# Gated linear attention beside routed experts: the state update with values stationary on column halves

## The reference, cut to what matters

```python
def step(state, inp):
    qt, kt, vt, at = inp
    state = at[..., None, None] * state + kt[..., None] * vt[:, :, None, :]
    out_t = jnp.einsum('bhk,bhkv->bhv', qt, state)
    return (state, out_t)
```

## Time and profile before

| what | value |
|---|---|
| time, median of 3 runs | 1334.08 us (1331.32 to 1335.56) |
| time of the profiled execution | 1335.15 us |
| its span (first to last instruction) | 1333.5 us |
| mean granted TensorE clock | 0.999 |

### The profile page before, as it was taken

One profiled execution on the slowest core, in us unless ns is written; L12 is line 12 of the kernel. 1 busy time (PEld: TensorE's weight loads), 2 busy tenths in 40 slices (PEclk: granted clock), 3 DMA queues, 4 the chain that ended last, 5 costly groups with the idle time before them and its releaser, 6 DMA issues.

```text
span 1333.5 us, 27468 instructions
## 1 busy us (share of the span) xinstructions
PE 1287.1 (97%) x9460; PEld 1128.6 (85%) x9460; DVE 956.0 (72%) x2431; ACT 550.2 (41%) x1075; POOL 484.4 (36%) x405
## 2 busy tenths in 40 slices
PE   6999999999999999899999999999999999999999
PEld 4888888888888887698888888988988989989887
DVE  6887878889796659866667577576675766757744
ACT  5665555556563433333333333333333333333322
POOL 1110100010010039626455456364554554545530
PEclk9999999999999999999999999999999999999999
DMA  6566534263352212246476476565765766656656
GB/s 228 188 232 185 182 110 164 91 198 116 131 179 73 80 48 80 77 117 150 114 181 162 103 196 133 141 157 122 174 159 109 190 128 159 155 127 157 159 154 229
DMA packets 124919, 194.66 MB, mean 146 GB/s; under 512 B 12016, under 2 KB 98608, under 8 KB 124592
## 3 DMA queue, kind: packets, MB, share of 16 engines
q1 hardware_dynamic: 94384, 147.99, 34.1%
q0 software_dynamic: 30464, 45.83, 19.2%
HBM read 148.62 MB, written 57.74 MB: 155 GB/s over the span
## 4 chain that ended last, share of the span: by engine, by line
PE 72%; DVE 14%; issue 6%; DMA 4%; POOL 2%; ACT 1%; DVEq 0%; SPq 0%; another core or an unknown queue 0%; POOLq 0%; ACTq 0%
PE bank L708 19%; PE bank L809 6%; PE bank L791 6%; PE bank L758 5%; PE bank L723 5%; PE bank L841 5%; PE bank L740 5%; PE bank L776 4%; PE bank L779 4%; PE bank L850 4%; DMA arena<-table,idx_all 3%; PE bank L749 3%; PE bank L831 2%; POOL sel_all L596 1%; PE bank L652 1%
## 5 line engine op out<-in xcount | busy, mean ns | idle before, releaser
L564 POOL DMA_INDIRECT arena<-table,idx_all x132 | 145.7, 1104 | 287.2 <-DVE arena L1458 256.1
L572 POOL DMA_INDIRECT acc<-arena,idx_all x128 | 211.4, 1651 | 43.8 <-issue 41.5
L708 PE MATMUL bank<-xp,wq 128*128 128x512 f32 x768 | 213.3, 413 | 0.0
L708 PE MATMUL bank<-xp,wk 128*128 128x512 f32 x768 | 204.7, 402 | 0.2 <-DVE wk L1274 0.2
L708 PEld LDWEIGHTS bank<-xp,wk 128*128 128x128 f32 x768 | 141.5, 189 | 34.5 <-DVE wk L1274 0.6
L708 PEld LDWEIGHTS bank<-xp,wq 128*128 128x128 f32 x768 | 139.9, 188 | 28.4 <-issue 0.5
L1353 DVE TENSOR_TENSOR_SCAN Dt<-decay,eye_b 128x512 f32<-128x512 f32 x128 | 158.0, 1236 | 0.8 <-issue 0.8
L1029 ACT ACTIVATE qT<-bank 128x512 f32<-128x512 f32 x128 | 76.6, 599 | 144.2 <-PE bank L708 137.4
L758 PE MATMUL bank<-qT,kT 128*128 128x128 f32 x1024 | 135.2, 275 | 0.0
L791 PEld LDWEIGHTS bank<-V,kw 128*128 128x128 f32 x960 | 117.7, 191 | 11.7 <-issue 9.8
L791 PE MATMUL bank<-V,kw 128*128 128x64 f32 x960 | 126.9, 275 | 0.0
(11 more groups left out here) (157 smaller groups left out, 2241.1 us busy)
## 6 DMA issues: line engine op xcount, KB each, us to landing
decay<-decay_dram SPq DMA_DIRECT2D x64, 512.0 KB
carry<-decay_dram SPq DMA_DIRECT2D x60, 512.0 KB, 4.5
arena<-in_L_attn_x_dram SPq DMA_DIRECT2D x16, 512.0 KB, 4.5
table<-arena SPq DMA_DIRECT2D x16, 512.0 KB, 3.4
xT_dram<-arena SPq DMA_DIRECT2D x16, 512.0 KB, 3.0
arena<-in_L_ffn_w_gate_dram SPq DMA_DIRECT2D x64, 128.0 KB
arena<-in_L_ffn_w_up_dram SPq DMA_DIRECT2D x64, 128.0 KB
arena<-in_L_ffn_w_down_dram SPq DMA_DIRECT2D x64, 128.0 KB
```

The lines of the kernel that those rows point to most:

```text
L564: pool.indirect_dma_start(out=xg[:, e % 2, j, :], out_offset=None, in_=table[:, :], in_offset=bass.IndirectOffsetOnAxis(ap=idx_all[:, e, j ...
L572: pool.indirect_dma_start(out=acc[:, :], out_offset=bass.IndirectOffsetOnAxis(ap=idx_all[:, e, j:j + 1], axis=0), in_=yb[:, e % 2, j, :], ...
L708: last = mm(to[:, :], w[:, part, k, h * DK:(h + 1) * DK], xp[:, other, k, :], start=(k + i == 0), stop=(k == KD - 1 and i == 2))
```

## The change

The update is done once for each pair, in the even slot, and turned. V (64 columns) is now stationary, on the column half of its head, and the weighted keys of both heads (`kw` now has room for two) move, 128 columns each. The sum of a pair comes out with values on partitions, in `bank[3]`. ScalarE copies it to SBUF (`update_copy`, into the half of `kw` that the second head has just left free), and TensorE transposes it back into `bank[6]` with four transposes (`update_back`). VectorE adds it as before, with the axes in another order.

On TensorE `update` stands ahead of `outputs`, `update_back` behind it; the odd slots have no update. In the steps "norm" (from step 1) and "count" the projection of the output gate (`proj_og`) moves from between the two projections of a head to behind them. On ScalarE `update_copy` stands behind the copy of the keys, ahead of place 2, except in the experts' steps, where it stands behind the hidden layer's gate, and the high parts of the next weights come after it.

```diff
-        kw = sb("kw", [P, B, DK])
+        kw = sb("kw", [P, 2, B, DK])
+        added_t = kw[:, 1, :, :]
...
                 if not (isinstance(c, int) and c == 0 and h == 0):
                     pe.wait_ge(kw_cp, at(c, 8, h))
+                    if h % 2 == 0:
+                        pe.wait_ge(ut_cp, at(c, 4, h // 2))
...
-            def update(c, h):
-                pe.wait_ge(kw_cp, at(c, 8, h + 1))
-                if h > 0 and h % 2 == 0:
-                    pe.wait_ge(state_up, at(c, 4, h // 2))
-                if h == 0 and not (isinstance(c, int) and c == 0):
+            def update(c, p):
+
+                pe.wait_ge(kw_cp, at(c, 8, 2 * p + 2))
+                pe.wait_ge(v_cp, 4 * c + 4)
+                for b in range(B):
+                    for u in range(2):
+                        h = 2 * p + u
+                        last = mm(bank[3][u * DV:(u + 1) * DV, b * P:(b + 1) * P], V[:, b, h * DV:(h + 1) * DV],
+                                  kw[:, u, b, :], start=True, stop=True)
+                last.then_inc(ut_ps, 1)
+
+            def update_back(c, p):
+
+                pe.wait_ge(ut_cp, at(c, 4, p) + 1)
+                if p > 0:
+                    pe.wait_ge(state_up, at(c, 4, p))
+                elif not (isinstance(c, int) and c == 0):
                     pe.wait_ge(wo_cp, 4 * c)
                 for b in range(B):
-                    lo = (h % 2) * B * DV + b * DV
-                    last = mm(bank[6][:, lo:lo + DV], kw[:, b, :], V[:, b, h * DV:(h + 1) * DV],
-                              start=True, stop=True)
-                if h % 2:
-                    last.then_inc(u_ps, 1)
+                    last = tr(bank[6][:, b * P:(b + 1) * P], added_t[:, b, :], ident[:, :])
+                last.then_inc(u_ps, 1)
...
-                    if s in og_slots(kind):
+                    og_first = first or in_turns(kind)
+                    if s in og_slots(kind) and og_first:
                         proj_og(c, kind, og_slots(kind).index(s))
...
                     if s < H:
                         proj_qk(c, kind, s, 1)
+                    if s in og_slots(kind) and not og_first:
+                        proj_og(c, kind, og_slots(kind).index(s))
                     beside(c, kind, s, 2)
+                    if s % 2 == 0 and not is_last(c):
+                        update(c, s // 2 - 1)
                     if s % 2 == 0:
                         outputs(c, s // 2 - 1)
                     beside(c, kind, s, 4)
-                    if not is_last(c):
-                        update(c, s - 1)
+                    if s % 2 == 0 and not is_last(c):
+                        update_back(c, s // 2 - 1)
                     beside(c, kind, s, 3)
...
+            def update_copy(c, p):
+                act.wait_ge(ut_ps, at(c, 4, p) + 1)
+                f(added_t.rearrange("p b d -> p (b d)"), bank[3][:, :], ACT.Copy).then_inc(ut_cp, 1)
...
-                    if s < H:
-                        weights_high_e(c, s)
+                if kind == "experts" and 0 < s < H and place == 3:
+                    weights_high_e(c, s)
...
+                    copied_last = s % 2 == 0 and kind == "experts"
+                    if s % 2 == 0 and not copied_last and not is_last(c):
+                        update_copy(c, s // 2 - 1)
...
                     beside(c, kind, s, 2)
+                    if copied_last:
+                        update_copy(c, s // 2 - 1)
+                    beside(c, kind, s, 3)
                     if s % 2 == 0:
                         outs_high(c, s // 2 - 1)
...
-                added = bank[6][:, :].rearrange("p (r v) -> p r v", v=DV)
+                summed = state[:, 2 * p:2 * p + 2]
+                added = bank[6][:, :].rearrange("p (b u v) -> p u b v", b=B, u=2)
...
-                tt(both, both, added, ALU.add).then_inc(state_up, 1)
+                tt(summed, summed, added, ALU.add).then_inc(state_up, 1)
```

More of the change, by code:

```diff
@@ L276, in build @@
         state_scaled, state_up = sem("state_scaled"), sem("state_up")
+        ut_ps, ut_cp = sem("ut_ps"), sem("ut_cp")
         gate_done, g_high, g_low = sem("gate_done"), sem("g_high"), sem("g_low")
@@ L801, in out_proj @@
                 if isinstance(c, int) and c == C - 1:
-                    pe.wait_ge((kw_cp, state_up)[b // 2], (8, 4)[b // 2] * (C - 1))
+                    pe.wait_ge((ut_cp, state_up)[b // 2], 4 * (C - 1))
                 elif b == 1:
@@ L972, in keys_weighted @@
                 for b in range(B):
-                    ins = f(kw[:, b, :], bank[3][:, b * P:(b + 1) * P], ACT.Copy, scale=Dt[:, h, b, P - 1:P])
+                    ins = f(kw[:, h % 2, b, :], bank[3][:, b * P:(b + 1) * P], ACT.Copy, scale=Dt[:, h, b, P - 1:P])
                 ins.then_inc(kw_cp, 1)
@@ L1367, in keys_weighted @@
                 dve.wait_ge(kt_ps, at(c, 8, h + 1))
-                tt(kw[:, :, :], bank[3][:, :].rearrange("p (b d) -> p b d", b=B),
+                tt(kw[:, h % 2, :, :], bank[3][:, :].rearrange("p (b d) -> p b d", b=B),
                    Dt[:, h, :, P - 1:P].broadcast_to([P, B, DK]), ALU.mult).then_inc(kw_cp, 1)
@@ L1400, in pair_state @@
                 both = state[:, 2 * p:2 * p + 2].rearrange("p u b v -> p (u b) v")
-                added = bank[6][:, :].rearrange("p (r v) -> p r v", v=DV)
+                summed = state[:, 2 * p:2 * p + 2]
+                added = bank[6][:, :].rearrange("p (b u v) -> p u b v", b=B, u=2)
                 if is_first(c):
                     dve.wait_ge(u_ps, at(c, 4, p) + 1)
-                    dve.tensor_copy(both, added).then_inc(state_up, 1)
+                    dve.tensor_copy(summed, added).then_inc(state_up, 1)
                     return
```

## The result

The changed kernel takes 1360.83 us (median of 4 runs, 1355.58 to 1361.55) against 1332.70 for the kernel before (1330.85 to 1335.56): 1.0203 times as long, 95% interval 1.0182 to 1.0224, 28 us slower. The forecast was 1360. The profiled execution took 1361.55 us, its span is 1359.9.

A forecast was written before the change was run, and what follows sets the result against it. TensorE, 97% busy, was taken as the bound, with waits on chains from its outputs through VectorE. Experts 15, norm 9, rest 2 - 1 + 1 made +26 us on 1335.15: 1361, as median 1360; range 1336 to 1380.

The forecast's parts named there:

- TensorE saves 0.35 a pair: On TensorE, even slot grows 2.84 to 3.32 us, odd slot loses 0.83; 60 pairs, 21 us less if TensorE alone counted.
- Transposes back 0.54: On TensorE, four transposes of the sum take 0.45 us plus 0.1 for leaving the column halves; could cost 0.45 to 1.1.
- one after another: Rival on TensorE: transposes do not overlap, 0.56 us more in some 32 pairs, +18 us, 1378 us; chance 0.02.
- Experts' steps +1.87 each, 15 us: Eight experts' steps: outputs end 0.88 us later, so gate, rows and gathered tokens come later and TensorE waits; bounds +8 to +20.
- X + 3.3: VectorE's gate in even experts' slots starts at X + 3.32 instead of X + 2.44; X is the hidden layer's end.
- It just fits: Experts' steps: weights' low part, behind ScalarE's copy and high part, runs 2.55 to 3.24 us after X, before the gate.
- The clock still full: Sign that the forecast is right: the clock stays at full speed in the changed kernel.
- Norm steps +2.3 each, 9 us: Norm steps 1 to 4: later gates and ScalarE's new copy lengthen each step; bounds for the four +4 to +14 us.
- The router's wait: Norm steps, slot 1: the removed update's 0.83 us becomes TensorE's wait for the copy the router needs, gain 0.
- +0.6: Norm steps, slot 2: outputs allow the gate only at 275.99 instead of 275.41, delaying TensorE's wait for the copy by 0.6 us.
- +1.7: Norm steps, slot 4: ScalarE's new copy ahead of tokens' second half, table load and gate makes all behind 1.7 us later.
- The rest, +2: Remaining steps: step 0 +2 us (keys' copy shows in odd slots), count -1, slots +1; step 15 has no update.

The follow-up runs named there:

- the run with the constant matmuls: Changed kernel plus five matmuls on constant data ahead of the tokens' transposes in slots 4 and 8 of the experts' steps; 1352.76 us.
- the late state: Changed kernel, experts' steps: a pair's state is brought up to date only in the next odd slot, behind the finished rows; 1343.38 us (kernel before likewise: 1326.64).
- the two moves: Last weight's matmuls ahead of tokens' transposes, finished rows ahead of tokens' low part, in experts' steps; added to the kernel before with state late: 1324.21 us.
- the version turned in the experts' steps alone with the moves: Kernel before with the update turned only in experts' steps, state late there, matmuls of the last weight and finished rows moved earlier in slots 2 to 7; 1331.64 us.

## Why the prediction was right, and where not

- **TensorE saves 0.35 a pair**: right. An even slot is 3.27 long (3.32 forecast), and a step's own work 1.3 to 1.5 us shorter.
- **Transposes back 0.54**: right, 0.50 for four. Four of the 275 ns that the Trainium skill gives (TensorE: Matmul & The Clock Gate, section Part 4: PE-mode transpose), one after another, would have made 1.1. The trace doesn't bear this out: one lasts 0.27 us, but four take 0.50.
- **Experts' steps +1.87 each, 15 us**: the mechanism is right. The gate comes 0.89 later, the waits grow where they were placed (step 11, slots 4, 6 and 8: 1.47, 0.51 and 1.92 us), and the same lateness appears when only the order changes. Over the steps it is 25.0 us more of waits less 8 x 1.4 = 11 of saving, 14 us, without the clock. Wrong is the place "X + 3.3" of the gate, 2.90 in fact: it was counted from a start that held 0.43 us of one execution, read as the time of a release. "It just fits", of the weights' low part behind the copy, came true: the gate follows it without idle time.
- **"The clock still full"**: wrong, the step of the forecast that failed. Half clock was put at nothing. Four of the stretches in the experts' steps follow waits that the change made; TensorE's own time in a step with one is some 1.6 us longer, and filling the waits gave 5 to 8 us back. The 10.24 us of half clock in step 0 lengthen that step too, but no other run here has them: the others have 3.41 or none.
- **Norm steps +2.3 each, 9 us**: too large. Steps 1, 2 and 4 grew by 0.82, 0.75 and 1.25 us, step 3 by 2.1 with half clock in it (1.4 without, in the run with the constant matmuls): 4.9 in all. The router's wait is as forecast (0.69 for 0.8, gain 0). "+0.6" for slot 2 was 0.1, in step 4 0.3: there the gate followed the outputs' start by 2.8 us before and by 2.0 now, so it had not hung on them. "+1.7" for slot 4 was 1.53 at the gate and 0.8 to 1.3 by slot 7. So the waits for L992's copy, forecast at some 20 us, rose from 9.1 to 11.2 only.
- **The rest, +2**: count -1.5 (-1 forecast), slots +2.2 (+1), step 0 +4.2 in the profile (+2), of which some 3 are clock, since it is +1.2 with the late state, where that stretch is 3.41 us.

Against the second profile of the kernel before, the changed kernel's is 31 us longer, of which some 11 are half clock. What the forecast did reckon with comes to about 20, not 26. That 1360 is met is in part luck: a clock loss that the forecast left out stands in for a norm term that was too large.

## What to carry to other kernels

A shorter instruction group ahead of the one that releases another engine's chain can cost more than it saves: count from the release, not from the busy time; moving a tuned kernel's old update ahead of its outputs alone cost 16 us. Before trusting a wait of a few tenths in one profile, take a second execution of the same kernel. And when a change makes waits of about 2 us on TensorE, price the clock as well: filling them with useless matmuls was worth 5 to 8 us here.

Faster than both kernels is the kernel before with the late state and the two moves, nothing turned: 1324.21 us.

## What was not expected of the hardware

- In one execution of the kernel before, the gate in slots 4 and 6 of the experts' steps started 0.7 us or more after the outputs' last matmul, with VectorE idle ahead of it in most; in its second execution 0.32. The cause is open.
- Waits of equal length were followed by half clock or not: four of the eight in slot 8 of the changed kernel (half clock began 0.5 to 1.3 us after such a wait ended), and not the one of 1.90 us in the version turned in the experts' steps alone with the moves, whose seven others were 1.4 to 1.8. What decides between them these runs don't show.
- The version with the late state alone took 1338.3 us in the profiled execution and 1343.3 to 1343.8 in the others at the same mean clock (0.996 to 0.997); only the first has a trace, so the 5 us are not located.
